# Eight-expert feed-forward layers: dense computation of all experts replaced by routed tiles that pass through DRAM

## The reference

```
shared_out = (silu(x @ Wsg.T) * (x @ Wsu.T)) @ Wsd.T          # hidden 352
scores     = softmax(x @ Wr.T)                                # 8 experts
w_full     = the two largest scores, 0 for the other six
g, u       = silu(x @ Wg[e].T), x @ Wu[e].T for all e         # hidden 176 each
out        = sum over e of w_full[e] * ((g * u) @ Wd[e].T) + shared_out
x = x + 0.5 * ffn(layernorm(x));  x = x + attention(layernorm(x));  x = x + 0.5 * ffn(layernorm(x))
```

## Time and profile before

| | |
|---|---|
| median of three executions | 1333.02 us |
| the profiled execution, its own time | 1331.98 us |
| its span, first to last instruction | 1330.2 us |
| granted clock of TensorE, mean | 0.952 |
| PE busy | 1151.1 us (87% of the span), 6681 matmuls |
| DVE busy | 894.1 us (67%) |
| POOL busy | 657.5 us (49%) |
| ACT busy | 545.4 us (41%) |
| DMA: read from HBM, mean rate | 63.64 MB, 56 GB/s |
| units 12 and 13 | 445.2 to 589.3 us |
| units 14 and 15 | 589.3 to 786.0 us |
| units 16 and 17 | 786.0 to 929.8 us |

### The profile page before, as it was taken

How to read it: one execution, slowest core, us unless ns; L and a number is a source line. 1 busy time by engine, 2 the same in 40 slices (tenths; PEclk the granted TensorE clock), 3 DMA queues, 4 the chain that set the end, 5 groups by cost and what they waited for, 6 DMA issues and landing times.

```text
span 1330.2 us, 21598 instructions
## 1 busy us (share of the span) xinstructions
PE 1151.1 (87%) x6681; PEld 981.4 (74%) x6681; DVE 894.1 (67%) x2247; ACT 545.4 (41%) x1225; POOL 657.5 (49%) x784
## 2 busy tenths in 40 slices
PE   5887467999789998997887889999499999999996
PEld 4766366877667787876676668778489998799995
DVE  4577776588878747567767765646766655656565
ACT  2354742210110223227757742322155555455552
POOL 5555725730443386863414348778444434344430
PEclk9888888999889999998998999999699999999998
DMA  5214021220000032322102113323111110111100
GB/s 166 67 49 149 26 76 56 84 95 1 1 1 28 22 97 80 95 80 48 40 13 48 40 58 97 97 77 109 63 40 32 39 32 25 48 32 40 39 8 32
DMA packets 31972, 74.07 MB, mean 56 GB/s; under 512 B 7136, under 2 KB 10464, under 8 KB 31456
## 3 DMA queue, kind: packets, MB, share of 16 engines
q1 hardware_dynamic: 29520, 70.43, 17.5%
q10 hardware_dynamic: 1872, 2.74, 0.6%
q0 software_dynamic: 512, 0.07, 0.0%
HBM read 63.64 MB, written 3.28 MB: 50 GB/s over the span
## 4 chain that ended last, share of the span: by engine, by line
PE 56%; DVE 23%; ACT 9%; issue 6%; POOL 3%; DMA 2%; SPq 0%; DVEq 0%; POOLq 0%; ACTq 0%
PE ps L227 18%; PE ps L228 16%; PE ps L229 16%; DVE a_ptl L1265 4%; ACT a_p L1210 4%; PE ps L1241 3%; DVE a_p L1202 2%; DVE x L1001 2%; ACT a_pth L1257 1%; DVE ffn_hl L702 1%; ACT ffn_hh L661 1%; PE ps L327 1%; PE ps L1026 1%; DVE xn L281 1%; DVE drl L1849 1%
## 5 line engine op out<-in xcount | busy, mean ns | idle before, releaser
L1228 POOL TENSOR_SCALAR a_p<-a_p,small 128x128 f32<-128x128 f32 (+3 forms) x256 | 131.4, 532 | 274.7 <-DVE small L1219 274.7
L227 PE MATMUL ps<-xh,wh 128*128 128x512 f32 x480 | 199.3, 415 | 9.7 <-POOL wl L418 5.2
L228 PE MATMUL ps<-xl,wh 128*128 128x512 f32 x480 | 194.0, 404 | 0.0
L229 PE MATMUL ps<-xh,wl 128*128 128x512 f32 x480 | 193.5, 403 | 0.0
L1210 ACT ACTIVATE a_p<-a_p,small 128x128 f32<-128x128 f32 (+3 forms) x256 | 141.7, 555 | 85.0 <-DVE small L1202 85.0
L387 POOL TENSOR_TENSOR wl<-raw,wh 128x384 fp32r<-128x384 f32 (+2 forms) x120 | 157.8, 1315 | 10.0
L385 POOL TENSOR_SCALAR wh<-raw 128x384 fp32r<-128x384 f32 (+2 forms) x120 | 75.4, 629 | 156.2 <-PE ps L229 156.1
L1265 DVE TENSOR_TENSOR a_ptl<-ps,a_pth 128x384 fp32r<-128x384 f32 (+1 forms) x192 | 106.5, 597 | 54.5 <-ACT a_pth L1257 54.3
L661 ACT ACTIVATE ffn_hh<-ffn_hf 128x512 fp32r<-128x512 f32 x88 | 55.5, 631 | 186.6 <-DVE ffn_hf L696 121.2
L418 POOL TENSOR_TENSOR wl<-raw,wh 128x512 fp32r<-128x512 f32 x88 | 117.3, 1333 | 7.3
L227 PE MATMUL ps<-wh,ffn_hh 128*128 128x256 f32 x352 | 105.4, 299 | 17.3 <-DVE ffn_hl L702 17.3
(11 more groups left out here) (308 smaller groups left out, 3065.1 us busy)
## 6 DMA issues: line engine op xcount, KB each, us to landing
raw<-in_w SPq DMA_DIRECT2D x56, 448.0 KB, 3.3
raw<-in_w SPq DMA_DIRECT2D x32, 384.0 KB, 3.1
raw<-in_qk SPq DMA_DIRECT2D x16, 512.0 KB, 3.5
raw<-in_v SPq DMA_DIRECT2D x16, 256.0 KB, 2.6
delta_table<-d_back SPq DMA_DIRECT2D x4, 528.0 KB, 4.5
d_back<-delta_table ACTq DMA_DIRECT2D x2, 1024.0 KB, 6.9
a_sq<-a_qh SPq DMA_DIRECT2D x64, 32.0 KB, 2.0
a_sk<-a_kh SPq DMA_DIRECT2D x64, 32.0 KB, 2.0
```

The costliest lines, as they stand in the source:

```text
L227: pe.matmul(o, l[0], r[0], start=start, stop=False, skip_group_check=True)
L228: pe.matmul(o, l[0], r[1], start=False, stop=False, skip_group_check=True)
L229: return pe.matmul(o, l[1], r[0], start=False, stop=stop, skip_group_check=True)
L1228: g.tensor_scalar(pp, pp, h_inv[:, par, i:i + 1], 1.0, ALU.mult, ALU.mult).then_inc(sem("at_norm"), 1)
```

## The change: routed experts as tiles through DRAM

Units 12 and 13 are now one piece of the program, 16 and 17 another (`pe_moe2` and so on do nothing for an odd unit). The shared expert stays dense: three chunks a batch (SH_CH), its weights loaded and split once and kept. The router finds the two experts of a row, a few matmuls with a triangle and with ones (`rank`) count the rows of each expert, and DVE computes for each of the 1024 pairs of a row and an expert its place in a list in which the rows of each expert begin at a multiple of 128 (`place`), and for each of the 15 tiles (NT) of the list the address of its expert's weights (`table`). POOL scatters the rows of xn to their places in DRAM (moe_x) by eight indirect DMAs a batch. Per tile SP loads 128 rows, PE transposes them, computes gate and up together (6 matmuls of 352 columns) with weights at an address that it reads into a register (`value_load`, L888), transposes the hidden rows, computes down (6 matmuls of 256 columns), ACT copies the result out and SP stores it in DRAM (moe_y). POOL gathers the two results of every row back by eight indirect DMAs a batch, and DVE adds them with their weights (`dve_combine`).

The expert weights (8 pieces of 128 x 1216, 622 KB each) are loaded whole into SBUF before unit 12 and split by ACT (high part, in units 10 and 11) and POOL (`expert_lo`, 128 x 1216 each, four before and four after the norm of unit 12). ATT2 uses their space, so POOL loads them again in heads 8 to 15 of unit 14, and they are split again inside the second piece: high parts on ACT, low parts of e = 0 to 2 on POOL, 3 to 7 on DVE. The gathers of unit 13 lie in the heads of unit 14, those of unit 17 ahead of the norm of unit 19. `wo3` is loaded after unit 15 and split on POOL in the second piece. The list in DRAM is zeroed at the start by SP. ATT2 has one buffer for v, filled again at head 8. Most semaphores are old ones that are used again (REUSED: rg_x is t_x, rg_clo t_xlo, rg_n t_h, rg_glo t_hlo, rg_gelu t_y, d_zeroed m_in3, d_sm r2_logits, d_scattered m_scat0, d_dest r2_pos, d_smt m_ahi).

```diff
-PLAIN2 = FS // P
-CH2 = -(-(E * FE + FS) // P)
+SH_CH = -(-FS // P)
+EW = 2 * DC * FE + 2 * D
+NT = (2 * T + E * (P - 1)) // P
...
+        def expert_lo(eng, m, e):
+            eng.wait_ge(*since("m_ahi", E * m + e + 1))
+            eng.tensor_tensor(expert(m_b, e), expert(m_raw, e), f32(expert(m_a, e)), ALU.subtract).then_inc(sem("m_blo"), 1)
...
+        def pe_moe2(pe, u):
...
+            def tile_x(n):
+                pe.wait_ge(*since(f"m_in{n % 4}", 16 * (n // 4 + 1)))
+                if n >= 2:
+                    pe.wait_ge(*since("t_xlo", n - 1))
+                for c in range(DC):
+                    last = pe.transpose(ps[:, 2 + n % 2, c * P:(c + 1) * P], m_xs[:, n % 4, c * P:(c + 1) * P], ident[:, :])
+                last.then_inc(sem("t_x"), 1)
+            def tile_gu(n, at):
+                pe.wait_ge(*since("t_xlo", n + 1))
+                if n >= 2:
+                    pe.wait_ge(*since("t_h", n - 1))
+                mm3c(pe, ps[:, 4 + n % 2, 0:2 * FE], [xt_slot(n, c) for c in range(DC)],
+                     [[t[:, bass.ds(at + c * 2 * FE, 2 * FE)] for t in (m_a, m_b)] for c in range(DC)]).then_inc(sem("t_gu"), 1)
+            def tile_h(n):
+                pe.wait_ge(*since("t_h", n + 1))
+                if n < n0 + 2:
+                    pe.wait_ge(*since("sh_res", TT * 2 * (m + 1)))
+                else:
+                    pe.wait_ge(*since("t_hlo", n - 1))
+                pe.transpose(ps[:, 6 + n % 2, 0:P], m_h[:, n % 2, 0:P], ident[:, :])
+                pe.transpose(ps[0:FE - P, 6 + n % 2, P:2 * P], m_h[:, n % 2, P:FE], ident[:, :]).then_inc(sem("t_hT"), 1)
+            def tile_down(n, at):
+                pe.wait_ge(*since("t_hlo", n + 1))
+                if n < n0 + 2:
+                    pe.wait_ge(*since("r2_pos", 2 * (m + 1)))
+                else:
+                    pe.wait_ge(*since("t_y", n - 1))
+                rows = [slice(0, P), slice(0, FE - P)]
+                mm3c(pe, ps[:, n % 2, 0:D],
+                     [[t[rows[c], n % 2, c * P:(c + 1) * P] for t in (m_hTh, m_hTl)] for c in range(2)],
+                     [[t[rows[c], bass.ds(at + (2 * DC * FE + c * D), D)] for t in (m_a, m_b)] for c in range(2)])\
+                    .then_inc(sem("t_down"), 1)
+            at = {}
+            def load(n):
+                j, b = n % NT, (n - n0) // NT
+                if j == 0:
+                    pe.wait_ge(*since("m_tabs", 2 * m + b + 1))
+                at[n] = pe.value_load(m_tab[0:1, b, j:j + 1], min_val=0, max_val=(E - 1) * EW)
+            for n in range(n0 - 1, n0 + N2 + 2):
+                if n + 1 < n0 + N2:
+                    load(n + 1)
+                    tile_x(n + 1)
+                if n0 <= n < n0 + N2:
+                    if n == n0:
+                        pe.wait_ge(*since("m_blo", E * (m + 1)))
+                    tile_gu(n, at[n])
+                if n0 <= n - 1 < n0 + N2:
+                    tile_h(n - 1)
+                if n0 <= n - 2:
+                    tile_down(n - 2, at.pop(n - 2))
+            pe.wait_ge(*since("t_y", n0 + N2))
+            pe_T(pe, u + 2)
...
+            def split(b, j):
+                if m == 1 and SH_CH * b + j < 4:
+                    for e in (0, 1):
+                        act_expert_hi(s, 1, 2 * (SH_CH * b + j) + e)
...
+            for n in range(n0 - 1, n0 + N2 + 2):
+                if n + 1 < n0 + N2:
+                    x_hi(n + 1)
+                if n0 <= n < n0 + N2:
+                    silu(n)
+                if n0 <= n - 1 < n0 + N2:
+                    h_hi(n - 1)
+                if n0 <= n - 2:
+                    y_out(n - 2)
+            act_T(s, u + 2)
...
+            dve_T(v, u + 1)
+            if m == 1:
+                expert_lo(v, 1, 3)
+            residual(0)
+            top(1)
+            chunk_h(1, 0)
+            index(1)
+            chunk_lo(1, 0)
+            chunk_h(1, 1)
+            chunk_lo(1, 1)
+            chunk_h(1, 2)
+            chunk_lo(1, 2)
+            place(1)
+            table(1)
+            if m == 1:
+                for e in range(4, E):
+                    expert_lo(v, 1, e)
+            residual(1)
+            weights()
+            for n in range(n0 - 1, n0 + N2 + 1):
+                if n + 1 < n0 + N2:
+                    x_lo(n + 1)
+                if n0 <= n < n0 + N2:
+                    h(n)
+                if n0 <= n - 1:
+                    h_lo(n - 1)
+                late = n - (n0 + NT)
+                if 5 <= late < 5 + TT:
+                    dve_combine(v, u, late - 5)
+                if 9 <= late < 9 + TT:
+                    dve_stats(v, u + 2, (late - 9,))
+            dve_norm(v, u + 2)
+            dve_T(v, u + 2)
+        def pool_scatter_x(g, u):
+            b, q = u % 2, MOE2_AT[u]
+            g.wait_ge(*since("r2_pos", q + 1))
+            g.wait_ge(sem("ln_xn"), TT * (u + 1))
+            g.wait_ge(sem("m_xzero"), 16 * 8)
+            for i in range(TT):
+                for k in range(2):
+                    c = 2 * i + k
+                    g.indirect_dma_start(out=xs[b][:, :],
+                                         out_offset=bass.IndirectOffsetOnAxis(ap=m_pos[:, b, c:c + 1], axis=0),
+                                         in_=xn[:, b, i, :], in_offset=None).then_inc(sem(f"m_scat{b}"), 16)
+        def pool_gather_y(g, u, half):
+            b, q = u % 2, MOE2_AT[u]
+            if half == 0:
+                for p in range(2):
+                    last = N2 * (q // 2) + NT * (b + 1)
+                    g.wait_ge(*since(f"m_out{p}", 16 * ((last + 1 - p) // 2)))
+                if b == 0:
+                    g.wait_ge(*since("sh_lo", SH_CH * 2 * (q // 2 + 1)))
+            for c in range(TT * half, TT * half + TT):
+                if 2 * TT * q + c >= 4:
+                    g.wait_ge(*since("m_comb", 2 * TT * q + c - 3))
+                g.indirect_dma_start(out=m_gath[:, c % 4, :], out_offset=None, in_=ys[b][:, :],
+                                     in_offset=bass.IndirectOffsetOnAxis(ap=m_pos[:, b, c:c + 1], axis=0))\
+                    .then_inc(sem(f"m_got{c % 4}"), 16)
+        def pool_moe2(g, u):
+            m = MOE2_AT[u] // 2
+            pool_ln(g, u + 1)
+            if m == 0:
+                units_done(g, u)
+                for t in (drh, drl):
+                    g.memset(f32(t[:, :]), 0.0).then_inc(sem("a2_vzero"), 1)
+            else:
+                for e in range(2):
+                    expert_lo(g, 1, e)
+            pool_scatter_x(g, u)
+            if m == 1:
+                expert_lo(g, 1, 2)
+            pool_scatter_x(g, u + 1)
+            if m == 1:
+                pool_wo3(g)
+            pool_gather_y(g, u, 0)
+            pool_gather_y(g, u, 1)
+            pool_ln(g, u + 2)
...
+        def sp_moe2(sp, u):
+            m = MOE2_AT[u] // 2
+            n0 = N2 * m
+            def load(n):
+                j, b = n % NT, (n - n0) // NT
+                if j == 0:
+                    sp.wait_ge(*since(f"m_scat{b}", 16 * 2 * TT * (m + 1)))
+                    sp.wait_ge(*since("r2_logits", 2 * (m + 1)))
+                if n >= 4:
+                    sp.wait_ge(*since("t_x", n - 3))
+                sp.dma_start(m_xs[:, n % 4, :], xs[b][j * P:(j + 1) * P, :]).then_inc(sem(f"m_in{n % 4}"), 16)
+            def store(n):
+                j, b = n % NT, (n - n0) // NT
+                sp.wait_ge(*since("t_y", n + 1))
+                sp.dma_start(ys[b][j * P:(j + 1) * P, :], m_y[:, n % 2, :]).then_inc(sem(f"m_out{n % 2}"), 16)
+            for n in range(n0, n0 + 4):
+                load(n)
+            for n in range(n0, n0 + N2):
+                if n + 4 < n0 + N2:
+                    load(n + 4)
+                store(n)
...
         def dve_ffn3(v, u):
...
+            if u == 18:
+                bias()
+                residual()
+                for t in range(TT):
+                    dve_combine(v, 17, t)
+                dve_stats(v, u + 1)
+                dve_norm(v, u + 1)
...
         def pool_att2(g, u):
...
+            if u == 14:
+                pool_gather_y(g, 13, 0)
             for h in range(H):
                 pool_norm(g, n0 + h, h % 2, a2_p)
+                if u == 14 and h == 2:
+                    pool_gather_y(g, 13, 1)
...
+                if u == 14 and h >= 8:
+                    units_done(g, 14)
+                    pool_expert(g, h - 8)
...
@@ -2028,40 +2599,33 @@
             pool_ln(g, 11)
-            some(12, pool_zero_a2, g, a2_vl[:, :, :, :], 10)
-            some(12, pool_zero_w, g, 10)
-            pre(12)
+            for e in range(4):
+                expert_lo(g, 0, e)
             pool_ln(g, 12)
-            rest(12)
-            pre(13)
-            rest(13)
-            some(12, pool_resident, g, "att2", 9)
-            some(14, pool_att2, g, 14)
-            some(15, pool_att2, g, 15)
-            pre(16)
-            some(16, pool_zero_w, g, 16)
-            rest(16)
```

(19 more changed lines are left out.)

781 lines of the change are left out of this document (547 added, 234 removed).

## The result

The changed kernel takes 1351.42 us (median of four executions, 1347.62 to 1357.52), the kernel before 1332.71 in the same comparison. The ratio is 1.0139, with a 95% interval of 1.0100 to 1.0177: slower, where I had forecast 1321 and faster. The profiled execution is the longest of the four, 1357.52 us with a span of 1355.7, so its segments hold some 6 us that a median execution doesn't have.

What follows compares the result with a forecast made beforehand. PE was taken to bound units 12, 13, 16 and 17. Terms -28.1 + 7.7 + 6 + 3 made -11.4 us, so 1331.98 became 1320.6, stated as 1321; forecast's own range 1303 to 1338, overall range 1285 to 1352.

Steps and rivals of the forecast that it cites:

- The net of -11.4: Whole kernel: 28.1 us gained in units 12, 13, 16, 17, less losses of 7.7, 6 and 3 elsewhere.
- A tile, 2.86 us by the ring: Tile loop: load n+5 waits behind store n, so copy, store issue, load and PE step take 5.6 to 5.7 us per two tiles.
- 25 x 2.9 for the whole loop: Each tile loop: five tiles at PE's 2.1 us, then 25 at 2.9, together 83 us.
- rival 4: Tile loops: PE's 0.75 us gaps drop the clock to 1.2 GHz, 4.2 us a tile, 1407 in all; chance 0.06.
- The heads, 38 and 44: Shared expert and routing ahead of the tiles: 38 us in units 12 and 13, 44 in units 16 and 17.
- and 1 because POOL's two memsets stand ahead of the scatter: Term in the first head's 38 us: 1 us for two POOL memsets standing before the scatter.
- Units 10 and 11, +3: POOL's low-part splits hold DVE's norms and accumulations in unit 11: loss 3 us, bounds 0 and 8.
- ATT2, +6: Units 14 and 15: second filling of v, gathers and combinations lose 6 us, bounds 0 and 12.
- Units 18 and 19, +7.7: Stretch from FFN3 to ATT3: storing the last tile, gathers and additions lengthen 25.5 us to 33.2, loss 7.7.
- The register load: PE reads each tile's weight address: taken as hidden in PE's 0.75 us idle time per tile, costing nothing.
- The range: Total time between 1285 and 1352 us, leaving out half of two rivals and all of the clock rival.
- rivals 2 and 3: Tile loops: register load stalls PE (1371 at 1.5 us), chance 0.12; row loads land late (1338 to some 1378), chance 0.12.

Runs made afterwards that it cites:

- the edits to the head: Six loads ahead, DVE zeroing, later POOL low parts, early combinations; added: DVE splits experts 4, 5 in gaps, first tile's low part before batch 1's residual: 1301.44 us.

## Why the prediction was wrong

The direction was wrong. The net of -11.4 was a difference between 28.1 us gained in the pieces and 16.7 lost outside. In the profile the pieces gained 5.7 and 31.6 were lost outside, of which 4.9 in units 0 to 9 are scatter. Of the 22.8 us that the pieces are longer than forecast, 12.6 lie in the heads and 10.2 in the loops with their ends. By its steps:

- **A tile, 2.86 us by the ring.** Right in mechanism, and in size (2.87) with luck. The terms as written add up to 5.58 us, 2.79 a tile, and errors cancelled in them: the store's issue 0.32 for 0.60, PE's step 2.5 for 2.1. The 0.2 for write latency and semaphores has no row; in the chain four pieces of 0.02 to 0.04 stand in its place. PE's missing 0.37 us are the change to 48 rows and back (0.19 is gone with 128 rows) and the register load with its arithmetic (0.15).
- **25 x 2.9 for the whole loop.** Failed in the second loop: 3.07 a tile. I had the fall of the clock as a rival for the whole loop (rival 4) at 0.06, against which stood that ATT2 has gaps as long and the same busy share, 0.82. By my own numbers the share in the loop was 2.1 of 2.86, 0.73. The fall came in pieces: behind two of the four waits over 1.5 us some tiles ran at the lower clock, and the second loop began at 0.58 behind the wait of 7.94. With the waits gone the window from 520 to 560 shows 1.00, and both loops run at 2.47.
- **The heads, 38 and 44.** This is the largest miss, and it alone is more than the forecast gain of 11.4: 45.0 and 49.6, 12.6 us over, counted as in the forecast from 3.8 us after the start of the transposes of unit 12 or 16 to the first gate matmul of a tile (501.05, 850.96). The step "and 1 because POOL's two memsets stand ahead of the scatter" priced what waits behind the memsets on POOL, not what DVE does beside them. The earlier trace rows had shown it, and I used it for units 10 and 11 but not here: PE waited 5.4 us, and with the memsets off POOL the head measured 37.0. In the second head I called POOL's splits parallel; the norm beside two of them took 6.39 us. DVE's own row of four took 5.4 us, near the 5.7 that I had; with residual and weights behind it PE waited 7.9, of which the edits to the head took 4.6 away (3.38 are left), and the second piece lost 5.0.
- **Units 10 and 11, +3.** Right in mechanism, 6.3 in size, within the bounds. The splits stand in both units and not in unit 11 alone; 5.3 of the 6.3 are in unit 11.
- **ATT2, +6.** 12.6 in this profile, just beyond the upper bound of 12; 8.0 to 12.6 in the six profiles with the same ATT2. Neither the combinations nor the second filling is shown to be the cause, and the mechanism of this loss stays open.
- **Units 18 and 19, +7.7.** Right (6.3).
- **The register load.** Right: hidden, by the runs too.
- **The range.** 1285 to 1352 contains the median of 1351.4, at its edge, and that is luck: its upper part stood for rivals 2 and 3, the register load and late loads, and neither came. The heads, which made most of the difference, had no bounds. The forecast's own upper bound was 1338, and even that is below what its parts give: 11 from the losses and 10 from the tiles make 1342.

The change itself does what it should: PE has less to do, and with its order mended the same idea takes 1289.6 us. The expected gain went into four places with a shown cause, a load queued behind a store, one-piece POOL instructions beside DVE, DVE work in a row ahead of the first tile, and the clock that some of the gaps take down, and into ATT2, where the cause is open.

## What to carry to other kernels

When tiles pass through DRAM on one queue, write down for each load which store stands before it and which result this store waits for; two loads further ahead were worth 30 us here, one less cost 206. Price a long POOL instruction by what DVE has to do while it runs, not only by what stands behind it on POOL, and look in the trace which of DVE's operations it holds. And when gains and losses are sums of many estimates, ask which way their errors lean: work that leaves a stage usually comes back at each handover.

## What the runs showed of the hardware

- A conversion of 128x8 on DVE took 5.79 us beside two POOL memsets of 3.95 in four profiles, 3.15 in one and 1.89 in two, and 0.17 without them; a norm of 128x256 took 1.96 to 2.90 us beside 128x1216 splits on POOL and 0.41 beside an idle POOL. Accumulations of 128x256 (L1517) took 0.48 us beside the same splits.
- Of four waits of 1.57 to 1.76 us on PE between tiles, two were followed by tiles at a lower clock (0.57 and 0.67) and two were not. The loops with all waits taken out kept 1.00 where I looked. That kernel's executions lie within 4.8 us, those of the four kernels with four loads ahead within 5.9 to 16.8; that the clock makes this difference is not shown.
- The first matmul on 48 rows after one on 128 took 0.31 us in the chain, where those behind it took 0.12; with 128 rows throughout it took 0.12 too.
- A register load on PE took 0.30 us and showed only in the period of a tile, as 0.15 us in the median, and only where the change of the row count did not cover it.
